# Query feature transposes of a linear-attention stage: a PSUM bank of their own, ScalarE copies, and split semaphores

## The reference

```python
def softmax_kernel(data, proj, is_query):
    data_n = data * d ** (-0.25)
    dd = jnp.einsum('bhnd,md->bhnm', data_n, proj)
    diag = 0.5 * jnp.sum(data_n * data_n, axis=-1, keepdims=True)
    if is_query:
        stab = jnp.max(dd, axis=-1, keepdims=True)
    else:
        stab = jnp.max(dd)
    return ratio * (jnp.exp(dd - diag - stab) + KERNEL_EPS)
```

## Time and profile before

| | |
|---|---|
| median of 3 runs | 906.93 us (904.53 to 907.21) |
| the profiled execution | 905.02 us |
| its span, first to last instruction | 903.3 us |
| PE, PEld, DVE, ACT, POOL busy | 704.9, 529.8, 650.5, 443.3, 262.3 us |
| mean granted TensorE clock, share of full | 0.89 |

### The profile page before, as it was taken

One profiled execution on the slowest core, in us unless ns is written; L12 is line 12 of the kernel. 1 busy time (PEld: TensorE's weight loads), 2 busy tenths in 40 slices (PEclk: granted clock), 3 DMA queues, 4 the chain that ended last, 5 costly groups with the idle time before them and its releaser, 6 DMA issues. The chain is left out here.

```text
span 903.3 us, 15196 instructions
## 1 busy us (share of the span) xinstructions
PE 704.9 (78%) x5016; PEld 529.8 (59%) x5016; DVE 650.5 (72%) x2828; ACT 443.3 (49%) x1051; POOL 262.3 (29%) x242
## 2 busy tenths in 40 slices
PE   3876977878718989888777588887776957878888
PEld 1436524433318777777675366544455956878888
DVE  5665565565559798986596466665538999999984
ACT  1112004345118877888674255555542555565562
POOL 3110221200143232232141121121003027776783
PEclk9886557798958999999888699999997979999999
DMA  8500052200089978898555343322000000000000
GB/s 251 136 1 2 12 64 39 34 6 2 1 308 354 397 275 339 307 397 319 198 194 146 107 54 48 42 38 39 3 1 1 1 1 1 5 4 4 4 8 7
DMA packets 42679, 93.68 MB, mean 104 GB/s; under 512 B 4050, under 2 KB 30194, under 8 KB 34408
## 3 DMA queue, kind: packets, MB, share of 16 engines
q0 software_dynamic: 9216, 69.47, 20.1%
q1 hardware_dynamic: 33384, 23.23, 13.1%
HBM read 74.42 MB, written 0.52 MB: 83 GB/s over the span
## 5 line engine op out<-in xcount | busy, mean ns | idle before, releaser
L742 ACT ACTIVATE arena<-arena,hact 128x128 f32<-128x128 f32 x512 | 155.0, 388 | 1.0
L565 POOL TENSOR_TENSOR arena<-arena 128x1024 f32<-128x1024 f32 x64 | 121.2, 1912 | 82.6 <-DVE arena L1216 65.2
L644 ACT ACTIVATE arena<-psum 128x512 f32<-128x512 f32 (+1 forms) x192 | 102.4, 562 | 81.2 <-PE psum L1366 80.0
L873 DVE TENSOR_REDUCE rowmax<-psum 128x2 f32<-128x512 f32 x128 | 81.5, 686 | 49.6 <-PE psum L1348 48.6
L1067 DVE CUSTOM_DVE_ANT_0 arena<-arena,fx 128x128 f32<-128x128 f32 x384 | 106.0, 344 | 0.3
L1683 PE MATMUL psum<-arena 128*128 128x128 f32 x688 | 86.8, 284 | 21.4 <-DVE arena L1216 19.2
L1572 PE MATMUL psum<-identf,arena 128*128 128x128 f32 x544 | 75.6, 294 | 27.9 <-ACT arena L742 27.3
L1683 PEld LDWEIGHTS psum<-arena 128*128 128x128 f32 x688 | 82.3, 197 | 25.0 <-DVE arena L1216 12.5
L1572 PE MATMUL psum<-arena,identf 128*128 128x128 f32 x544 | 79.5, 304 | 15.3 <-ACT arena L742 14.6
L795 ACT ACTIVATE psum<-arena,tneg 128x1024 f32<-128x1024 f32 x64 | 71.0, 1111 | 39.8 <-POOL arena L565 14.1
L1572 PEld LDWEIGHTS psum<-identf,arena 128*128 128x128 f32 x544 | 68.6, 203 | 35.1 <-ACT arena L742 24.7
(11 more groups left out here) (215 smaller groups left out, 1235.3 us busy)
## 6 DMA issues: line engine op xcount, KB each, us to landing
arena<-parts SPq DMA_DIRECT2D x144, 64.0 KB
arena<-zeros SPq DMA_DIRECT2D x6, 1232.0 KB
w_sb<-attn_w SPq DMA_DIRECT2D x1, 768.0 KB, 8.1
x<-x_in SPq DMA_DIRECT2D x1, 512.0 KB, 4.4
fx<-ctx_in SPq DMA_DIRECT2D x1, 512.0 KB, 5.4
picked<-mask_in SPq DMA_DIRECT2D x1, 512.0 KB, 6.9
wq_sb<-peer_wq SPq DMA_DIRECT2D x1, 512.0 KB, 7.1
down_sb<-table_down SPq DMA_DIRECT2D x1, 512.0 KB, 7.8
```

Of the source, the lines that this page charges most:

```text
L565: nc.gpsimd.tensor_tensor(grid[k % 3].rearrange("p (i j) -> p i j", i=PK), sim[:, t, h, :].unsqueeze(2).to_broadcast([P, PK, PK]), sim[:, ...
L644: nc.scalar.activation(probs[k % (2 * HG)][:, 0:w], bank(2 + k % 2, 0, w), ACT.Exp, scale=float(D) ** -0.5).then_inc(probs_ready, 1)
L742: a = nc.scalar.activation(w, w, ACT.Copy, scale=hact[i % 2][:, l:l + 1])
L873: i = nc.vector.tensor_reduce(rowmax[n % 2][:, :, h], bank(k % 2).rearrange("p (s n) -> p s n", s=SUB), AX.X, ALU.max)
```

## The change

The query transposes no longer go into banks 0 and 1 but into bank 6, one half s at a time (`turn_q`), and ScalarE, not VectorE, copies each half to `qf_t`. The feature matmuls are cut into `features(n, 0)` (queries, raises the new `ddq_ps`, waits for `zq_ready` of the batch before) and `features(n, 1)` (keys, raises `dd_ps`, waits for `zk_ready`), with `half_norms` (raises the new `hn_ps`) between them. TensorE's order for a batch becomes: projections of n + 1, query features of n + 1, first turn of n, half norms and key features of n + 1, second turn of n. VectorE waits for `ddq_ps`, `hn_ps` and `dd_ps` each where it needs it. `qft_ps` and `qft_ready` now count halves. The context transposes wait for `qft_ready` as well, since the second half of them goes into bank 6.

```diff
--- before.py
+++ after.py
@@ -198,6 +198,7 @@
         cols_ps, probs_ready, pv_ps = sem("cols_ps"), sem("probs_ready"), sem("pv_ps")
         o_ready, ot_ps, ot_ready = sem("o_ready"), sem("ot_ps"), sem("ot_ready")
         y_ps, x_ready = sem("y_ps"), sem("x_ready")
+        ddq_ps, hn_ps = sem("ddq_ps"), sem("hn_ps")
         sq_ready, dd_ps, zq_ready, zk_ready = sem("sq_ready"), sem("dd_ps"), sem("zq_ready"), sem("zk_ready")
         eq_ready, qft_ps, qft_ready = sem("eq_ready"), sem("qft_ps"), sem("qft_ready")
         kmax_ready, kmax_all, nkmax_ready = sem("kmax_ready"), sem("kmax_all"), sem("nkmax_ready")
@@ -476,7 +477,7 @@
 
                 pool.wait_ge(qk_ready, n + 1)
                 if n >= 1:
-                    pool.wait_ge(dd_ps, n)
+                    pool.wait_ge(hn_ps, n)
                 nc.gpsimd.tensor_tensor(sq[:, :, :], qk_f[n % 2][:, :, :], qk_f[n % 2][:, :, :], ALU.mult).then_inc(sq_ready, 1)
 
             def split(n):
@@ -651,8 +652,12 @@
                     evac_qkv(n + 1)
                 act.wait_ge(zq_ready, n + 1)
                 if n >= 1:
-                    act.wait_ge(qft_ps, n)
+                    act.wait_ge(qft_ps, SUB * n)
                 nc.scalar.activation(eq, zq, ACT.Exp).then_inc(eq_ready, 1)
+                for s in range(SUB):
+                    act.wait_ge(qft_ps, SUB * n + s + 1)
+                    nc.scalar.activation(qf_t[:, SUB * n + s, :, :], bank(6).rearrange("p (g n) -> p g n", g=HG),
+                                         ACT.Copy, bias=1e-4).then_inc(qft_ready, 1)
 
             for half in range(2):
                 act.wait_ge(ctxt_ps, half + 1)
@@ -902,7 +907,7 @@
             for n in range(B):
                 if n + 1 < B:
                     norm(n + 1)
-                dve.wait_ge(dd_ps, n + 1)
+                dve.wait_ge(ddq_ps, n + 1)
                 if n >= 1:
                     dve.wait_ge(eq_ready, n)
                 ddq = psum[:, 0:2 * BANK].rearrange("p (g m) -> p g m", m=M)
@@ -910,9 +915,11 @@
                 half_norm = bank(7, 0, 64).rearrange("p (w s h) -> p w (s h)", w=2, s=SUB)
                 sv = stab[:, :, :].rearrange("p s h -> p (s h)")
                 link(nc.vector.tensor_reduce(sv, ddq, AX.X, ALU.max))
+                dve.wait_ge(hn_ps, n + 1)
                 link(nc.vector.tensor_tensor(sv, half_norm[:, 0, :], sv, ALU.add))
                 nc.vector.tensor_tensor(zq.rearrange("p (g m) -> p g m", m=M), ddq,
                                         sv.unsqueeze(2).to_broadcast([P, 2 * H, M]), ALU.subtract).then_inc(zq_ready, 1)
+                dve.wait_ge(dd_ps, n + 1)
                 nc.vector.tensor_reduce(kmax[:, SUB * n:SUB * n + SUB],
                                         psum[:, 2 * BANK:4 * BANK].rearrange("p (s c) -> p s c", s=SUB), AX.X, ALU.max)
                 dve.wait_ge(zq_ready, n + 1)
@@ -920,10 +927,6 @@
                 nc.vector.tensor_tensor(zk[:, SUB * n:SUB * n + SUB, :].rearrange("p s (g m) -> p (s g) m", m=M), ddk,
                                         sv.unsqueeze(2).to_broadcast([P, 2 * H, M]), ALU.subtract).then_inc(zk_ready, 1)
                 dve.wait_ge(zk_ready, n + 1)
-                dve.wait_ge(qft_ps, n + 1)
-                nc.vector.tensor_scalar(qf_t[:, SUB * n:SUB * n + SUB, :, :],
-                                        psum[:, 0:2 * BANK].rearrange("p (s g n) -> p s g n", s=SUB, g=HG),
-                                        1e-4, None, ALU.add).then_inc(qft_ready, 1)
                 if n < B - 1:
                     split_bias(nc.vector, link, (4 + 2 * n) * P, min(6 + 2 * n, 9) * P)
             nc.vector.tensor_copy(bias_w[:, 0:1], bias_p[:, 0:1]).then_inc(bias_ready, 1)
@@ -1401,38 +1404,58 @@
             pe.wait_ge(bias_ready, 1)
             pre_qk(0)
             pre_v(0)
-            for n in range(B):
+            def features(n, w):
+
+                if n == 0 and w == 0:
+                    pe.wait_ge(feat_ready, 1)
                 if n >= 1:
-                    pe.wait_ge(qft_ready, n)
-                    pe.wait_ge(zk_ready, n)
-                else:
-                    pe.wait_ge(feat_ready, 1)
+                    pe.wait_ge(zk_ready if w else zq_ready, n)
                 pe.wait_ge(qk_ready, n + 1)
                 fw = feat_w[:, :, :].rearrange("p h m -> p (h m)")
-                for w in range(2):
-                    for s in range(SUB):
-                        nc.tensor.matmul(bank(2 * w + s), qk_f[n % 2][:, w, s * P:s * P + P], fw, start=True, stop=True)
+                for s in range(SUB):
+                    i = nc.tensor.matmul(bank(2 * w + s), qk_f[n % 2][:, w, s * P:s * P + P], fw, start=True, stop=True)
+                i.then_inc(dd_ps if w else ddq_ps, 1)
+
+            def half_norms(n):
+
                 pe.wait_ge(sq_ready, n + 1)
+                if n >= 1:
+                    pe.wait_ge(zk_ready, n)
                 for w in range(2):
                     for s in range(SUB):
                         j = (w * SUB + s) * H
                         i = nc.tensor.matmul(bank(7, j, j + H), sq[:, w, s * P:s * P + P], half16[:, :], start=True, stop=True)
-                i.then_inc(dd_ps, 1)
+                i.then_inc(hn_ps, 1)
+
+            def turn_q(n, s):
+
+                pe.wait_ge(eq_ready, n + 1)
+                if n + s >= 1:
+                    pe.wait_ge(qft_ready, SUB * n + s)
+                for g in range(HG):
+                    j = (s * HG + g) * P
+                    i = nc.tensor.transpose(bank(6, g * P, g * P + P), eq[:, j:j + P], identf[:, :])
+                i.then_inc(qft_ps, 1)
+
+            features(0, 0)
+            half_norms(0)
+            features(0, 1)
+            for n in range(B):
                 if n + 1 < B:
                     pre(n + 1)
-                pe.wait_ge(eq_ready, n + 1)
-                for s in range(SUB):
-                    for g in range(HG):
-                        j = (s * HG + g) * P
-                        i = nc.tensor.transpose(psum[:, j:j + P], eq[:, j:j + P], identf[:, :])
-                i.then_inc(qft_ps, 1)
+                    features(n + 1, 0)
+                turn_q(n, 0)
+                if n + 1 < B:
+                    half_norms(n + 1)
+                    features(n + 1, 1)
+                turn_q(n, 1)
 
             def keys_values(n):
 
                 pe.wait_ge(kf_ready, n + 1)
                 if n == 0:
                     pe.wait_ge(zk_ready, B)
-                    pe.wait_ge(qft_ready, B)
+                    pe.wait_ge(qft_ready, SUB * B)
                     pe.wait_ge(v_ready, B)
                 elif n >= 2:
                     pe.wait_ge(cx_ready, n - 1)
```

## The result

The changed kernel takes 895.18 us (median of 4 runs, 892.72 to 896.68), the kernel before 906.06 (4 runs): a ratio of 0.9885, 95% interval 0.9863 to 0.9906. In the profiled executions it is 896.68 against 905.02, and spans of 894.9 against 903.3.

A forecast was written before the change was run, and what follows sets the result against it. One ring of TensorE, VectorE and ScalarE through shared banks bounds the stage; key exponential 77.42 to 64.25 gains 13.2 us, giving 891.9 from the profiled 905.02, 893.8 by the median; 892.8 taken, range 889.5 to 899.0.

The forecast's parts named there:

- The start of batch 0: First row-maximum no longer waits for half norms and key features: 22.9 us in place of 26.89.
- the 11.17 us of VectorE's list: VectorE's work per batch without the copy, 11.17 us, sets the pace in place of 13.73.
- the slack of TensorE in batches 1 and 2: TensorE's 9.4 us list fits in the 11.17 period; batch 1's query features ready 3 us early.
- the ring through banks 0 and 1: Before, transposes shared the features' banks, so next features waited for VectorE's copy: 13.73 us a batch.
- the mark: Start of the first key exponential, which ends the feature stage; predicted at 64.25 us against 77.42.
- no later: GpSimd's squares wait for half norms, which now precede key features, so they were expected no later.
- rival A: TensorE falls to the low clock before the last batches and is late: 893.5 to 898 us, chance 0.18.
- The tail: Batch 3 after the query subtraction: exponential, two turns, copies and context transposes in one bank, 57.0 to 64.25 us.
- rival C: Turns at the end run at the high clock, saving 1.6 us: 890.3 us, chance 0.14.
- One for one to the end: Nothing downstream waits for a fixed moment, so the 13.2 us gained at the key exponential reaches the end.
- Rivals B and D: B: low clock all stage, TensorE the bound, 912 us, chance 0.04. D: gain given back or banks' dependence stays, 905, 0.02.

The follow-up runs named there:

- late splits: Changed kernel with the three bias splits moved out of VectorE's feature loop to where VectorE waits anyway; 891.30 us, ratio 0.9883 to the kernel before.
- ScalarE alone: Kernel before with only the copy of turned query features moved to ScalarE, with banks, order and semaphores as before; 903.02 us, ratio 0.9997.
- the bank with VectorE's copies: Changed kernel with the two copies of turned query features back on VectorE, keeping bank 6 and split semaphores; 908.27 us, ratio 1.0040 to the kernel before.
- one common wait: Changed kernel with query and key features waiting together for the key subtraction, half norms after both; 895.51 us, ratio 0.9891 to the kernel before.
- the other two executions: The changed kernel run again without edit, twice, as yardstick; medians 894.97 and 894.36 us, ratios 0.9886 and 0.9896 to the kernel before.
- filled gap: Changed kernel with 16 unread transposes in TensorE's idle stretch ahead of batch 3's projections; 894.22 us, ratio 0.9874 to the kernel before.
- the one try: Changed kernel with context transposes moved earlier, four ahead of batch 3 and four between the last query turns; 890.14 us, ratio 0.9853 to the kernel before.

## Why the prediction held, and where it didn't

The start of batch 0, the 11.17 us of VectorE's list as the new pace, and the slack of TensorE in batches 1 and 2 held. Row-maxima were predicted at 22.9, 35.4, 46.6 and came at 23.35, 35.61, 46.82. ScalarE's copies are 0.60 each. The late splits confirm the pace. ScalarE alone gains next to nothing, and the bank with VectorE's copies nothing either: the ring through banks 0 and 1 is broken only by the bank together with an engine that doesn't stand in the way. With both and one common wait the mark is 5.5 us earlier than before (71.87 for 77.42), and the split semaphores bring the other 5.2.

**Batch 0 came out by two errors that cancel.** The key subtraction ended at 28.82, 0.6 before its forecast, and then the split took 4.0 us for 3.26. One of its instructions is the difference:

```profile
29.35 1.04 POOL L481 TENSOR_TENSOR sq<-qk_f 128x512 f32<-128x512 f32 x1 [9.29 <-ACT qk_f L603]
...
29.48 1.19 DVE L265 TENSOR_TENSOR arena<-arena 3x256 f32<-3x256 f32 x1
```

The same instruction takes 0.41 at 31.52, and 0.41 in the kernel before. It is long where GpSimd's squares run beside it, 1.19 here, 1.14 and 1.19 in the other two executions; in the kernel before the squares fell on other work of VectorE (29.98, 44.62 and 58.35), and the prediction let them pass as "no later". In batch 3 the first instruction of the split took 0.68 beside the squares, for 0.20. No run moved the squares, so that they are the cause is read from the overlap alone.

Two readings of rows were off as well. I priced two feature matmuls at the low clock as half of the 6.51 us of four, but the clock rose within those four; two alone took 3.78 in this execution. And the DMA share of the second slice is 5 tenths, not 2; the third is 0, so nothing hangs on it.

**Batch 3 was mis-sized.** The prediction had TensorE idle 0.9 us before its projections, since I let its list end at 45.7. It ended at 44.84, because TensorE was through with the turns of batch 0 (at 35.2) before the norm of batch 2 came at 35.6, where I had it 0.9 us behind the norm, and the idle stretch was 2.00. I took the high clock there; it was the low one each time. This is rival A, in its milder form, since the clock rose again before the key features (1.96). Fourth row-maximum 56.45 for 54.3, and the query subtraction ended at 59.99 for 57.0: 3.0 us. The filled gap removes all of it. The Trainium skill's rule (TensorE: Matmul & The Clock Gate, "A second HAM failure mode: psum-queue depth-cycling") names short stops from cycling through PSUM. The trace agrees with it only in that a stop goes ahead of the fall: from 22 to 45 us, with the same cycling and stops of at most 0.47, the clock was 1.00, and in batch 3 the fall came behind one stop of 2.00 us for VectorE's norm, and not when that stop was filled. I gave rival A 0.18, which was too little.

**The tail** came out near its sum by two errors that cancel. From the end of the last query subtraction to the key exponential I had 7.25; it took 7.63. The exponential started 1.2 us late, because on ScalarE it stands behind the copy of batch 2's second turn, which TensorE had made late (60.72): that queue I had passed over as free. The last turns then ran near the high clock, 0.65 and 0.63 for 0.95 in the sum, which is rival C in part; the context transposes behind them took 1.94 for eight, low as in the sum. So the tail's sum is near by luck: 1.2 lost, 0.8 gained.

**One for one to the end.** The gain at the key exponential was 9.8 for 13.2 predicted; the median's 10.9 is as near to it as the scatter allows. Over the thirteen profiled executions of this study, all kernels and variants together, the time from the key exponential to the end is 820.4 to 829.1 us, with no clear trend against the key exponential from 57 to 82. So the gain passes through on average, but in one execution nothing under some 5 us can be read from the span. In the medians it passes through unevenly: late splits and the filled gap are 6 and 4 us earlier at the mark than the changed kernel and about 1 us better in the time. I had taken 2.7 us of difference between runs as the scatter; the 43 runs of the kernel before in the three groups lie between 896.99 and 908.28.

Rivals B and D didn't happen. That half norms wait for the key subtraction cost nothing: where TensorE stood in the loop, it was for the norm (0.44 and 2.00), or 0.47 for ScalarE's copy of the turned rows, as before.

## What to carry to other kernels

When two engines exchange buffers in a ring, price the consumer's place in its list before its duration: the same copies cost little on an engine with slack (1.2 us of delay at the end) and 11 us on one that had the next norm behind them, by estimate 7 of it through the low clock behind the stops they made. After a stage has been rearranged, look at the longest idle stretch of TensorE that is left, since what follows it may run at half speed. Filling it with useless work gave 3.7 us at the mark; that useful work moved into it pays as well was not shown, since the one try, 0.60 us of it, was too little to hold the clock. And judge an edit of a few microseconds by a mark at the end of its stage, not by the span alone.

## What was not expected of the hardware

A single program differs by 6.4 us in one stretch, and the granted clock differs with it. The first cross attention (first row-maximum to first leaf product) took 139.2, 135.8 and 132.8 us in three executions. The stretch from 85 to 100 us behind the first row-maximum in the second and the first of the changed kernel's executions:

```profile
198.50:213.50 15.00, 11.65 (x102) 5.19 (x101) 5.64 (x21) 8.72 (x17) 0.00 (x0) 0.77 0.01 3
```

```profile
199.20:214.20 15.00, 13.04 (x125) 6.12 (x116) 5.79 (x24) 9.87 (x18) 0.81 (x1) 0.93 0.01 3
```

0.77 against 0.93, and more of TensorE's instructions done in the same time. The third execution has 0.93 there as well and is 3.0 us shorter still, so this stretch alone doesn't order the three. From 15 to 60 us behind the first row-maximum the clock does: 0.74, 0.80 and 0.88 for 139.2, 135.8 and 132.8 us, and 0.78 for the 138.4 of the kernel before. That the clock is the cause is argued from this order, since no run held the level fixed, and what sets the level from one execution to the next stays open.

That 0.6 us of work in a 2 us stop did not keep the clock up and 1.9 us of it did is measured once each.
